# The shared expert of a two-layer mixture-of-experts kernel, cut into 32 steps that run behind attention heads and beside the router

## The reference, cut to what matters

```python
# layer 0 attention (16 heads of 16, keys and values from a context of 64 rows), sigmoid and not softmax
scores = jax.nn.sigmoid(jnp.einsum('blhd,bshd->bhls', q, k))
o = jnp.einsum('bhls,bshd->blhd', scores, v).reshape(B, L, E)
x = x + jnp.tanh(g_xattn[0]) * (o @ Wo.T)
# layer 0 feed-forward on u = layernorm(x)
probs = jax.nn.softmax(u @ gate_w.T)            # 8 experts, the best 2 of each token, weights made to sum to 1
h = gelu(einsum('th,ehf->tef', u, W1) + b1)     # 256 -> 1024, per expert
y = einsum('tef,efh->teh', h, W2) + b2          # 1024 -> 256
sh = gelu(u @ sW1 + sb1) @ sW2 + sb2            # the shared expert: every token
x = x + jnp.tanh(g_ffn[0]) * (sum of the two y by weight + sh)
# layer 1: linear attention with a layer norm behind it, then 8 experts, no shared one
```

## Time and profile before

| | |
|---|---|
| Median of 3 runs | 843.84 us (841.26 to 844.49) |
| The profiled execution | 843.57 us, span 840.6 us |
| PE busy | 699.5 us (83%) |
| PE weight loads busy | 581.2 us (69%) |
| DVE, ACT, POOL busy | 501.3 us (60%), 450.7 us (54%), 333.2 us (40%) |
| Chain that ended last | PE 52%, DVE 17%, DMA 14%, ACT 6%, issue 6% |
| Transfers | 78.36 MB, 93 GB/s in the mean |

### The profile page before, as it was taken

One profiled execution on the slowest core, in us unless ns is written; L12 is line 12 of the kernel. 1 busy time (PEld: TensorE's weight loads), 2 busy tenths in 40 slices (PEclk: granted clock), 3 DMA queues, 4 the chain that ended last, 5 costly groups with the idle time before them and its releaser, 6 DMA issues.

```text
span 840.6 us, 22396 instructions
## 1 busy us (share of the span) xinstructions
PE 699.5 (83%) x7462; PEld 581.2 (69%) x7463; DVE 501.3 (60%) x1296; ACT 450.7 (54%) x1065; POOL 333.2 (40%) x251
## 2 busy tenths in 40 slices
PE   3788767989998899999999915663199999999994
PEld 3433323956667899998899914552189999999993
DVE  4645646425713677777555466995667777765552
ACT  1544473365555677777556531211086787765661
POOL 1112242234452444553455326642034544454442
PEclk9766575999999999999999967665599999999998
DMA  9610000050012556667445353001545666533332
GB/s 294 214 50 0 1 26 25 2 177 26 26 38 92 143 138 141 135 144 203 92 100 102 41 136 109 25 26 54 136 108 124 145 145 148 134 67 50 45 44 23
DMA packets 60919, 78.36 MB, mean 93 GB/s; under 512 B 5948, under 2 KB 48710, under 8 KB 60375
## 3 DMA queue, kind: packets, MB, share of 16 engines
q1 hardware_dynamic: 45814, 57.11, 21.4%
q0 software_dynamic: 15072, 20.84, 16.2%
HBM read 57.44 MB, written 20.50 MB: 93 GB/s over the span
## 4 chain that ended last, share of the span: by engine, by line
PE 52%; DVE 17%; DMA 14%; ACT 6%; issue 6%; POOL 1%; SPq 1%; POOLq 0%; DVEq 0%; ACTq 0%
DMA x_sum<-x_arena,add_now 10%; PE bank L995 6%; PE bank L996 6%; PE bank L997 6%; PE bank L1008 5%; PE bank L1010 5%; PE bank L1009 5%; PE bank L755 2%; DVE ln_stats L1391 2%; PE bank L733 2%; PE bank L756 2%; PE bank L757 2%; DMA x_arena<-token_rows,gather_now 2%; PE bank L978 1%; DVE weights L1530 1%
## 5 line engine op out<-in xcount | busy, mean ns | idle before, releaser
L1264 ACT ACTIVATE work<-bank,b_cols 128x128 f32<-128x128 f32 x624 | 177.7, 369 | 133.3 <-PE bank L997 128.4
L995 PE MATMUL bank<-x_arena,weights 128*128 128x128 f16 x1248 | 215.4, 220 | 3.6 <-DVE weights L1384 2.1
L996 PE MATMUL bank<-x_arena,weights 128*128 128x128 f16 x1248 | 215.3, 219 | 0.0
L997 PE MATMUL bank<-x_arena,weights 128*128 128x128 f16 x1248 | 215.0, 218 | 0.0
L1008 PE MATMUL bank<-weights,work 128*128 x624 | 170.2, 273 | 0.1
L1009 PE MATMUL bank<-weights,work 128*128 x624 | 170.2, 273 | 0.0
L1010 PE MATMUL bank<-weights,work 128*128 x624 | 170.2, 273 | 0.0
L1599 DVE TENSOR_TENSOR work<-work 128x512 f16<-128x512 f32 x156 | 101.0, 689 | 112.7 <-ACT work L1272 112.7
L995 PEld LDWEIGHTS bank<-x_arena,weights 128*128 x1248 | 120.0, 96 | 4.3 <-issue 2.3
L996 PEld LDWEIGHTS bank<-x_arena,weights 128*128 x1248 | 122.0, 98 | 0.0
L997 PEld LDWEIGHTS bank<-x_arena,weights 128*128 x1248 | 120.7, 97 | 0.0
(11 more groups left out here) (208 smaller groups left out, 1220.1 us busy)
## 6 DMA issues: line engine op xcount, KB each, us to landing
raw<-in_L_ffn_W SPq DMA_DIRECT2D x104, 256.0 KB
token_rows<-row_arena SPq DMA_DIRECT2D x2, 2072.0 KB, 10.4
weights<-in_L_ffn_W SPq DMA_DIRECT2D x16, 256.0 KB, 5.0
x_arena<-in_x SPq DMA_DIRECT2D x4, 512.0 KB, 6.0
weights<-in_L_ffn_sW SPq DMA_DIRECT2D x8, 256.0 KB, 7.2
x_sum<-x_arena SPq DMA_DIRECT2D x4, 512.0 KB, 2.8
x_arena<-in_L_ffn_b SPq DMA_DIRECT2D x2, 1024.0 KB, 9.3
row_arena<-in_L_ffn_W SPq DMA_DIRECT2D x8, 256.0 KB, 3.7
```

Of the source, the lines that this page charges most:

```text
L995: nc.tensor.matmul(o, w1_at[f][c][0].block(), hi, start=c == 0, stop=False)
L996: nc.tensor.matmul(o, w1_at[f][c][0].block(), lo, start=False, stop=False)
L997: m = nc.tensor.matmul(o, w1_at[f][c][1].block(), hi, start=False, stop=c == DC - 1)
L1264: m = nc.scalar.activation(hid[:, k, f * P:f * P + P], h_ps[k][half][:, g * P:g * P + P], ACT.Gelu, bias=b1_cols[n][:, f, bass.ds(e, 1)], ...
```

## The change

The shared expert keeps 32 steps, but a step is now 256 tokens and two blocks of hidden features (`CHUNKS` = 8 times `PAIRS` = 4). Steps 0 to 6 run behind head pairs 1 to 7 of batch 2, steps 7 to 14 behind the eight of batch 3, steps 15 to 31 after attention. The layer norm, the turn and the logits of each batch (now on `xln0` and `xlnT0`) run there too, and the pair of the turned rows is made from the router's own turn, so the f16 turns (L911) are gone. `second_keys` moves into batches 0 and 1 (head pairs 7, 9, 11, 13, 15), and the 12 splits into batches 0 and 1 (before: all four). Sigmoid becomes tanh, by sigmoid(z) = 0.5 + 0.5 tanh(z/2): the values' sum over the context (`value_sums`, 8 f32 matmuls of one column) is added at the read-out of `values`, and the factor 0.5 is in the gate of the attention. The combine weights too come from one tanh. `values` now uses one bank for both halves.

```diff
+        CHUNKS, PAIRS = T // (2 * P), FC // 2
+        STEPS = CHUNKS * PAIRS
+        LAG = 2
+        SHARED_FROM = 17
+        IN_ATTENTION = B * HP - SHARED_FROM
+        RESULTS = (22, 26, 30)
+        SECOND_KEYS = (7, 9, 11, 13, 15)
+        PROJECT3, ROUTE3, LOGITS3, COUNTS = 17, 21, 22, 27
+        POST_ROWS2, POST_LN3, POST_ROWS3 = 16, 19, 23
...
-        AHEAD = 8
+        AHEAD = 4
...
             for b in range(B):                                   # PE
                 pe.wait_ge(q_ready, b + 1)
                 for h in range(HP):
+                    n = HP * b + h
                     scores(b, h)
-                    if h == 0:
-                        transposed(b + 1)
+                    if h == 0 and b >= 2:
+                        router_turn(b - 2)
...
+                    if h == 2 and b < B - 1:
+                        transposed(b + 1)
...
+                    if n in SECOND_KEYS:
+                        second_keys(SECOND_KEYS.index(n))
+                    if n >= SHARED_FROM:
+                        shared_step(n - SHARED_FROM)
+                    if h == 1 and b >= 2:
+                        logits(b - 2)
...
+            router_turn(2)
+            for m in range(IN_ATTENTION, STEPS):
+                if m == 4 * PAIRS:
+                    values(B - 1, 1)
+                    logits(2)
+                if m == PROJECT3:
+                    project(B - 1)
+                if m == ROUTE3:
+                    router_turn(3)
+                if m == LOGITS3:
+                    logits(3)
+                if m == COUNTS:
+                    router_counts(0)
+                shared_step(m)
+            for m in range(STEPS - LAG, STEPS):
+                shared_down(m)
+            row_table(0)
...
+            def shared_high(m):                                  # ACT
+                first = 2 * (m % PAIRS)
+                act.wait_ge(s_up_done, m + 1)
...
+                for f in (first, first + 1):
+                    rows = slice(f % 2 * 2 * P, (f % 2 + 1) * 2 * P)
+                    g = nc.scalar.activation(s_hid[:, m % SRING, rows], s_h_ps[m % 2][:, rows], ACT.Gelu, bias=b1_cols[0][:, f, E:E + 1],
+                                             scale=1.0 / W_SCALE)
...
-                    nc.scalar.activation(probs[:, n % 2, :], s_ps[h % 2][:, :], ACT.Sigmoid, scale=float(DH) ** -0.5)
+                    nc.scalar.activation(probs[:, n % 2, :], s_ps[h % 2][:, :], ACT.Tanh, scale=0.5 * float(DH) ** -0.5)
...
             for b in range(B):                                   # DVE
                 attention0(b)
-            for c in range(DC):
-                o_low(B - 1, c)
-            third = norm_begin(6)
+            o_low(B - 1, 0)
+            s_x_low(2)
+            o_low(B - 1, 1)
+            keep_logits(2)
             add_attention0(B - 1)
             last = norm_begin(7)
-            norm_end(6, third)
+            shared_result(3)
             norm_end(7, last)
-            second_keys(0)
-            second_keys(1)
+            add_bias(3)
+            shared_result(4)
+            s_x_low(3)
+            keep_logits(3)
             pick_experts(0)
-            second_keys(2)
+            shared_result(5)
             row_words_of(0)
-            shared_result(0)
             place_rows(0)
-            shared_result(1)
+            shared_result(6)
             row_tokens(0)
-            shared_result(2)
-            shared_result(3)
+            shared_result(7)
             ffn(0)
```

More of the change, by code:

```diff
@@ new lines, in shared_down @@
+                for f in (first, first + 1):
+                    w_hi, w_lo = (weights[:, SHARED, w2_place(f, l):w2_place(f, l) + D] for l in range(2))
+                    for t in range(2):
+                        y, at = s_y_ps(i)[:, t, :], f % 2 * 2 * P + t * P
+                        hi, lo = (s_pair[:, m % SRING, l, at:at + P] for l in range(2))
+                        nc.tensor.matmul(y, lo, w_hi, start=f + t == 0, stop=False)
+                        nc.tensor.matmul(y, hi, w_hi, start=False, stop=False)
+                        d = nc.tensor.matmul(y, hi, w_lo, start=False, stop=f == FC - 1 and t == 1)
```

551 lines of the change are left out of this document (303 added, 248 removed).

## The result

The changed kernel is slower, by 0.8%: 851.74 us median (843.64 to 856.29) against 843.43 (838.55 to 849.13) for the kernel before in the same comparison, ratio 1.0081, 95% interval 1.0051 to 1.0110. The forecast was 826.6. Its profiled execution took 853.4 us with a span of 851.3; that of before had 843.57 and 840.6. The changed kernel's twenty runs fall into two groups, six at 843.6 to 845.8 us (granted clock of the whole run 0.890 to 0.897) and fourteen at 849.0 to 856.3 (0.880 to 0.894); the profiled one is of the second group.

The account below looks back on a forecast made before the run. PE bounds the shared expert; chains between engines, not throughput, bound attention. Terms -27.9 + 10.2 + 1.3 - 1.3 = -17.7, taken as 17, gave 843.6 - 17 = 826.6 us; 819 to 837 at chance 0.58, range 812 to 846.

Parts of the forecast that it names:

- batch 1: Second attention batch: key products +5.0, projection wait grows some 1.5, clock -2.5; taken as +4 us, bounds +0 and +10.
- Batch 0: First attention batch: first key product 4.15 and values' sums 1.85 use up a 3.17 wait; +2.8 us, splits covered.
- Batch 2: Third attention batch with seven shared steps: 31.7 of work, 6.1 of waits, 3.6 for low clock; 41.4 us.
- Batch 3: Fourth attention batch with eight shared steps: 33.2 of work, 4 of waits, 1 for the clock; 38.2 us.
- the rest as above: Batch 3's waits besides step 10's `down` (about 1.8), taken as in batch 2, within 4 us in all.
- After attention: From attention's end to PE's last shared block, 17 steps and routing: 56.6 of work, 4 of waits; 60.6 us.
- The start: Time before batch 0: no change forecast, batch 0 taken to start at 30.4 us as before.
- The tail: PE's last shared block to first expert tile: 1.6 + 10.0 + 0.9 = 12.5 us, against 2.3 before.
- rival 2: Head pairs with shared steps couple: about 1 us more wait in each of 15 pairs, +15, 842 us; chance 0.12.
- rival 4: Tanh not in Gelu's table: 30 loads of 1.28 us make ACT bind, about 850 us; chance 0.02 with the like.
- Rival 1: Clock stays low behind the heads in batches 2 and 3: +50 us throughout, +25 (851) for half; chance 0.11.
- 27.9 us: Gain at PE's last shared block, 234.3 against 262.2, from filled waits, the clock and dropped f16 turns.

Follow-up runs that it names:

- fill_clock: Changed kernel plus 14, 19 and 17 unread PE products ahead of the second and third key products and step 0: 846.04 us, ratio 1.0047 to the kernel before.
- keys_first: Changed kernel with DVE's three key pieces moved ahead of the low halves of heads 8, 10 and 16: 840.74 us, ratio 0.9982 to the kernel before.
- results_first: Changed kernel with DVE reading shared results 0 to 2 ahead of `o_low`, `norm_end` and `add_bias`: 844.62 us, ratio 1.0015 to the kernel before.
- before_tanh: Kernel before with Tanh written for Sigmoid in four places, without the factors, so not the reference's function: 838.82 us, ratio 0.9970.
- keys_results: Changed kernel with the edits of keys_first and results_first together: 833.19 us, ratio 0.9898; second comparison 833.73 us, 0.9916.
- early tail: Changed kernel with counts at step 25, row table before the last two down blocks, shared result 5 amid DVE's placing: 847.42 us, ratio 1.0053.
- all_fill: keys_results with the early tail, plus 9 unread products behind the first queries and 13 ahead of step 0: 825.59 us, 0.9793; again 823.87 us, 0.9801.
- half_fixed: keys_results with 8 shared steps in attention (`SHARED_FROM` 24 for 17) and splits spread over 23 heads: 832.7 us, ratio 0.9897 to the kernel before.

## Why the prediction was wrong

**The term that failed first: batch 1** (+4 forecast, +12.2 measured, outside its bound of +10). I priced the key products by PE's time at full clock (+5.0) and one wait, the 2.31 us before the projection, which "moves ahead and grows by some 1.5", so 3.8 in all. Every product but the last has a DVE or ACT piece between it and the one before, and I put only the mask (L1448) beside what stands in front of it in DVE's program. That wait was 4.65. The same wait one product earlier, for the bias sums (L1441), stood at nothing in my sum and was 4.94. And for the clock I took 2.5 us off, where it cost: fill_clock shows that 4.2 to 4.4 us of batch 1 are the clock. keys_first took both waits away by order alone, and batch 1 fell by 6.4 to 6.6 us.

**Batch 0** (+2.8 forecast, +1.5 measured) came out near by luck. I wrote that the splits "have cover". They have not: the crowded splits hold `head_values` back, PE waits 5.50 us for it, and with the splits spread batch 0 takes 26.8 us in place of 30.5. Against that the batch ran at 0.78 of the clock, where before had 0.60.

**Batch 2** (41.4, measured 46.7). Step 0 waited 4.15 in place of 2.7, as DVE's copies of the fifth product were the later of its two conditions, which I had not listed; with 2.02 for the projection's bank and 1.33 for the queries the waits come to 7.5 in place of 6.1. The low clock at its head cost more than the 3.6 I gave it: a mean of 0.85 over 46.7 us is 14 us at the low level, 1.5 of them inside the wait, so by my estimate some 6 us. With the fill ahead of step 0 the batch takes 42.8 to 44.5, 2.4 to 5.0 less than without.

**Batch 3** (38.2, measured 42.9). Step 10's `down` waited 2.00 against 1.8; step 14's, 3.44, I had left in "the rest as above". With 0.88 for the projection's bank that makes 6.3 in place of 4. DVE's norm took 3.11 us there beside a busy POOL. results_first removes both waits. The eight head pairs add 1.4, at 3.47 us in place of 3.3.

**After attention** (60.6, measured 64.7): the waits, 1.83 for the kept logits and 2.31 for the last turn, add up to my 4, though I had them in part elsewhere. What I did not count is a clock of 0.97, which is 3.9 us at the low level and some 2 us of loss; 2 us more are spread over the stage in small pieces.

**The start** (+2.7) was chance: first tanh from 31.4 to 34.0 in nineteen profiles, with both dealings of banks.

**The tail** (12.5 forecast, 14.0 measured) was right in kind. PE waited 1.52 us for the row table (forecast 1.6). The gathers take longer than layer 1's: from the first gather's issue to the first turn 3.86 us against 2.99, and the second turn comes 2.8 us behind the first against 1.2. From the first turn to the end the changed kernel took 582.6 us against 578.2; layer 1 gained 1.4 by its table loads as forecast (from row table to the end 240.5 against 241.9), so layer 0's tiles lost some 3 more than I had: from the first turn to the last one of layer 0 it is 216.1 us against 211.3. The versions of the changed kernel with results_first's edit lie at 577.5 to 579.8 from first turn to end, those without at 580.4 to 582.6. Why was not tested.

**What held.** The moved work does fit behind the heads at the price named: a head pair with a step takes 3.47 us (177.38 to 180.85) against 3.3, without the coupling of rival 2: no L958 or L973 but those of steps 0, 10 and 14 has a wait of 0.7 us or more. The Gelu and tanh share a table (rival 4 wrong): the changed kernel has loads at 0.72 and 109.32 only. ScalarE: Activation LUTs in the Trainium skill names tanh in other sets than gelu's ("Table sets: the hidden batching unit"). This trace, with two loads in place of the 30 worked out from that list, contradicts it, and so does before_tanh, which has two where before has five. Rival 1, the low clock, was the right kind of danger, but with a cause I had not given it: it was low behind the DVE waits (0.70 in batch 1) and high where PE ran with few waits, 0.97 in batch 3. The forecast said 17 us less than before. Order alone, both waits cured, gives 7 to 9 us less (keys_results), and with the early tail 10.5 to 11. The forecast's 826.6 is reached only with fills: all_fill has 825.6, with 205.1 us (203.3 in its second profile) from first tanh to last shared block, where the forecast has 234.3 - 31.4 = 202.9. That agreement is luck and hides three errors. It needs the early tail, 4.2 us that the forecast did not count on, and 22 products that nothing reads, 5.7 us. And the sum rests on all fifteen steps alike, while half_fixed is as fast with eight of them. The 27.9 us that I wanted from PE's last block came to 4.4 in the changed kernel.

## What to carry to other kernels

When work is moved in front of others' instructions, write down for each product what its read-out stands behind on the reading engine and what that waits for: in batch 1 DVE idled for 5.39 us before one instruction while the input of a later one was ready, and PE waited 4.94 us for that. Read-outs that a producer needs go ahead of work that waits for a third engine. Look at the queues of the stage that takes in moved side work too, here the splits in batch 0. And price a gap of PE of 2 to 5 us at more than its length, as a range: in batch 1 nearly half as much again (4.4 us on 9.6) was lost to the clock behind it, while behind a gap of 2.00 us it was nothing in one execution and some us in another.

## What was not expected of the hardware

The same gap of 2.00 us was followed by a granted clock of 1.00 in one execution and 0.66 in another, at a cost of a few us. DVE's norm (L1482, 4 x 128x256) takes longer the more POOL is busy inside it: 1.38 us with POOL idle, 2.31 with POOL busy for 1.15 of it (217.86), 2.52 with 1.9 (keys_results, 135.71) and 3.11 with 2.47 (184.70). In the changed kernel's order of time, with POOL idle:

```profile
83.04 1.38 DVE L1482 TENSOR_SCALAR work<-x_arena,ln_mv,ln_rstd 128x256 f32<-128x256 f32 x4
```

and the ten us around the slow one (POOL is the fifth engine):

```profile
180.00:190.00 10.00, 6.56 (x51) 4.38 (x49) 6.00 (x8) 6.23 (x13) 8.86 (x7) 1.00 0.00 1
```

Tanh and Gelu alternate 15 times without a table load; the one load of 1.28 us stood, all but 0.2 us, under PE's wait before step 0.
